# An LSTM step in which the residual part of h comes from a scan, the whole h is formed on GpSimd, and the output gate's sums change places

## What is computed

```
xW = einsum('ntd,dg->ntg', x, Wx) + b           # g = 2048 columns: i, f, o, g
a = xw_t + prev_h @ Wh
i, f, o = sigmoid(a[:, 0:H]), sigmoid(a[:, H:2H]), sigmoid(a[:, 2H:3H]);  g = tanh(a[:, 3H:])
next_c = f * prev_c + i * g
next_h = o * tanh(next_c)
x = x + hs
```

## Time and profile before

| what | value |
|---|---|
| median of three runs | 7913.7 us (7913.2 to 7918.02) |
| the profiled execution: its own time | 7913.46 us |
| its span | 7911.4 us |
| TensorE busy | 5366.3 us (68%) |
| VectorE busy | 5627.1 us (71%) |
| ScalarE busy | 2281.7 us (29%) |
| GpSimd busy | 842.9 us (11%) |
| granted TensorE clock in the LSTM steps (500 to 4000 us) | 1.00 |

### The profile page before, as it was taken

One profiled execution on the slowest core, in us unless ns is written; L12 is line 12 of the kernel. 1 busy time (PEld: TensorE's weight loads), 2 busy tenths in 40 slices (PEclk: granted clock), 3 DMA queues, 4 the chain that ended last, 5 costly groups with the idle time before them and its releaser, 6 DMA issues. The chain is left out here.

```text
span 7911.4 us, 404450 instructions
## 1 busy us (share of the span) xinstructions
PE 5366.3 (68%) x169280; PEld 4157.3 (53%) x169280; DVE 5627.1 (71%) x37427; ACT 2281.7 (29%) x12741; POOL 842.9 (11%) x2143
## 2 busy tenths in 40 slices
PE   1566666666666666666983666666666666666666
PEld 1455555555555555555431555555555555555555
DVE  7777777777777777777678777777777777777776
ACT  4322222222222222222354222222222222222222
POOL 5100000000000000000013000000000000000000
PEclk5899999999999999999996999999999999999999
DMA  2000000000000000000001000000000000000001
GB/s 85 17 0 0 0 0 0 0 0 0 0 0 0 0 0 0 0 0 0 0 0 43 0 0 0 0 0 0 0 0 0 0 0 0 0 0 0 0 0 43
DMA packets 32261, 37.24 MB, mean 5 GB/s; under 512 B 6112, under 2 KB 22496, under 8 KB 32224
## 3 DMA queue, kind: packets, MB, share of 16 engines
q1 hardware_dynamic: 32224, 36.76, 1.4%
HBM read 28.34 MB, written 8.39 MB: 5 GB/s over the span
## 5 line engine op out<-in xcount | busy, mean ns | idle before, releaser
L404 PE MATMUL q_PA<-scratch,q_H 128*8 128x256 f16 (+1 forms) x32768 | 1255.2, 273 | 1071.8 <-DVE q_H L619 1071.8
L404 PE MATMUL p_PA<-scratch,p_H 128*8 128x256 f16 (+1 forms) x32768 | 1254.9, 273 | 1071.8 <-DVE p_H L619 1071.8
L404 PEld LDWEIGHTS q_PA<-scratch,q_H 128*8 128x8 f16 (+1 forms) x32768 | 649.7, 90 | 1494.2 <-DVE q_H L619 1359.7
L404 PEld LDWEIGHTS p_PA<-scratch,p_H 128*8 128x8 f16 (+1 forms) x32768 | 649.0, 90 | 1494.6 <-DVE p_H L619 1359.6
L404 PE MATMUL q_PB<-scratch,q_H 128*8 128x256 f16 (+1 forms) x32768 | 1249.7, 273 | 0.0
L404 PE MATMUL p_PB<-scratch,p_H 128*8 128x256 f16 (+1 forms) x32768 | 1249.4, 273 | 0.0
L593 DVE STREAM_TRANSPOSE q_GT<-q_PA 128x192 f32<-128x192 f32 (+1 forms) x2048 | 526.0, 295 | 747.7 <-PE q_PA L404 747.7
L593 DVE STREAM_TRANSPOSE p_GT<-p_PA 128x192 f32<-128x192 f32 (+1 forms) x2048 | 526.5, 295 | 746.7 <-PE p_PA L404 746.7
L404 PEld LDWEIGHTS q_PB<-scratch,q_H 128*8 128x8 f16 (+1 forms) x32768 | 834.5, 92 | 59.8
L404 PEld LDWEIGHTS p_PB<-scratch,p_H 128*8 128x8 f16 (+1 forms) x32768 | 833.5, 92 | 60.8
L492 ACT ACTIVATE q_GBA<-q_PREA 128x24 f32<-128x24 f32 x1024 | 194.7, 190 | 1900.9 <-DVE q_PREA L598 1900.9
(11 more groups left out here) (220 smaller groups left out, 9390.6 us busy)
## 6 DMA issues: line engine op xcount, KB each, us to landing
scratch<-in_x_dram SPq DMA_DIRECT2D x8, 1024.0 KB, 5.4
out_dram<-xa SPq DMA_DIRECT2D x16, 512.0 KB, 6.1
xb<-in_L_cond_Wx_dram SPq DMA_DIRECT2D x8, 384.0 KB, 6.8
xb<-in_L_cond_Wh_dram SPq DMA_DIRECT2D x8, 384.0 KB, 6.7
xa<-in_L_cond_Wx_dram SPq DMA_DIRECT2D x8, 384.0 KB, 5.9
xa<-in_L_cond_Wh_dram SPq DMA_DIRECT2D x8, 384.0 KB, 6.1
xb<-in_L_cond_Wx_dram SPq DMA_DIRECT2D x8, 128.0 KB, 7.0
xb<-in_L_cond_Wh_dram SPq DMA_DIRECT2D x8, 128.0 KB, 6.8
```

The source lines that it names most:

```text
L404: last = nc.tensor.matmul(half.banks[buf][Q * j:Q * j + rows, 0:GA * Q], H[:, u, k, 0:rows], w16[:, part, k, j, half_cols(half)], start=False,
```

## The change

The sums of the output gates change places. The first half's o and the second half's g, i, f are neighbours in GT, and the two `both_parts` on them (8 and 24 elements) become one with 32, into one PSUM bank (PREB); the sigmoid of the first half's o now waits for it. The second half's o is transposed and summed ahead of the first half's high part, into PREA, with a wait for the transposition between the two (`to_b`).

`whole_h` leaves VectorE. The sigmoid of o and tanh of c are now written by ScalarE into one SBUF tile SO, in triples of which the first element is 0, the second the sigmoid and the third tanh of c; the element that was in PSUM before (tanh of c) is in SBUF now. H becomes HP, also in triples with -128 in the first element. `low_h` is a scan over 24 elements in place of an operation on 8: its state is multiplied by SO and HP is subtracted, so that after the first element of a triple it is 128, after the second 128 o, and after the third 128 o tanh(c) minus the high part. The matmuls read the third elements, 12 bytes apart, instead of adjacent columns. GpSimd multiplies the two parts of SO of four steps into HH, waits for that, and then adds HH to x.

The diff, without the renamed memsets, the allocation of the semaphores and the rewritten arguments of the calls:

```diff
-        H = sbt("H", [P, V, NC, Q], F16)
-        HH = sbt("HH", [P, 2, V, NC * B])
+        HP = sbt("H", [P, 2, V, V, 2, B, NF, 3], F16)
+        SO = sbt("SO", [P, U, 2, B, NF, 3])
+        HH = sbt("HH", [P, V, NC * B])
...
-                self.tanh_c = pst("TC" + name)[:, 0:M]
-                self.sig_o = sbt("SIGO" + name, [P, M])
+                self.n = chunk // NF
+                self.sig_o, self.tanh_c = (SO[:, :, self.n, :, :, e].rearrange("p u b c -> p u c b") for e in (1, 2))
...
+        first.pre_o, pre_o_and_gif, o_and_gif = second.pre[:, 0:M], second.pre[:, 0:4 * M], (first.o[0], second.gif[1])
+        second.pre_o = first.pre[:, 3 * M:4 * M]
...
-                    nc.gpsimd.tensor_tensor(here, here, HH[:, v].rearrange("p u (c b) -> p c u b", b=B), ALU.add).then_inc(s["xadd"], 1)
+                    nc.gpsimd.tensor_tensor(HH[:].rearrange("p u (h c b) -> p (u h) b c", h=2, b=B),
+                                            *(SO[:, v * V:(v + 1) * V, :, :, :, e].rearrange("p u h b c -> p (u h) b c") for e in (1, 2)), ALU.mult).then_inc(s["whole"], 1)
+                    pool.wait_ge(s["whole"], done)
+                    nc.gpsimd.tensor_tensor(here, here, HH[:].rearrange("p u (c b) -> p c u b", b=B), ALU.add).then_inc(s["xadd"], 1)
...
-                    last = nc.tensor.matmul(half.banks[buf][Q * j:Q * j + rows, 0:GA * Q], H[:, u, k, 0:rows],
+                    last = nc.tensor.matmul(half.banks[buf][Q * j:Q * j + rows, 0:GA * Q], HP[:, k // NF, u, 0:u + 1, :, :, k % NF, 2].rearrange("p u s b -> p (u s b)"),
...
-            nc.vector.memset(H[:], 0.0).then_inc(s["zero"], 1)
+            nc.vector.memset(HP[:].rearrange("p h s u t b c e -> p (h s u t b c) e")[:, :, 0], -H_SCALE).then_inc(s["zero"], 1)
+            nc.vector.memset(HP[:].rearrange("p h s u t b c e -> p (h s u t b c) e")[:, :, 1:3], 0.0).then_inc(s["zero"], 1)
...
-            def whole_h(half, v, u):
-                return nc.vector.tensor_tensor(HH[:, v, u, half.cols], half.sig_o[:], half.tanh_c, ALU.mult)
...
-                nxt = next_h(half, u)
-                return nc.vector.scalar_tensor_tensor(nxt[:, :, B:2 * B], by_unit(HH[:, v, u, half.cols]), H_SCALE, nxt[:, :, 0:B],
-                                                      ALU.mult, ALU.subtract)
+
+                here = (u + 1) % V
+                threes = lambda a: a.rearrange("p b c e -> p (b c e)")
+                return nc.vector.tensor_tensor_scan(threes(HP[:, half.n, here, here, 1]), threes(SO[:, v * V + u, half.n]),
+                                                    threes(HP[:, half.n, here, here, 0]), 0.0, ALU.mult, ALU.subtract)
```

More of the change, by code:

```diff
@@ L493, in steps @@
                                              scale=half_scale).then_inc(s["g_a"], 1)
-                        act.wait_ge(s["preo_a"], now)
-                        nc.scalar.activation(first.sig_o[:], first.pre_o, ACT.Sigmoid, scale=scale)
+                        act.wait_ge(s["pre_b"], now)
+                        nc.scalar.activation(first.sig_o[:, u], by_unit(first.pre_o), ACT.Sigmoid, scale=scale)
                         act.wait_ge(s["c_a"], now)
-                        nc.scalar.activation(first.tanh_c, first.c, ACT.Tanh, scale=0.5).then_inc(s["tc_a"], 1)
-                        act.wait_ge(s["pre_b"], now)
+                        nc.scalar.activation(first.tanh_c[:, u], by_unit(first.c), ACT.Tanh, scale=0.5).then_inc(s["tc_a"], 1)
                         nc.scalar.activation(second.tanhs, second.pre_gif.rearrange("p (n m) -> p n m", n=3), ACT.Tanh,
@@ L501, in steps @@
                         act.wait_ge(s["preo_b"], now)
-                        nc.scalar.activation(second.sig_o[:], second.pre_o, ACT.Sigmoid, scale=scale)
+                        nc.scalar.activation(second.sig_o[:, u], by_unit(second.pre_o), ACT.Sigmoid, scale=scale)
                         act.wait_ge(s["c_b"], now)
-                        nc.scalar.activation(second.tanh_c, second.c, ACT.Tanh, scale=0.5).then_inc(s["tc_b"], 1)
+                        nc.scalar.activation(second.tanh_c[:, u], by_unit(second.c), ACT.Tanh, scale=0.5).then_inc(s["tc_b"], 1)
             act.wait_ge(s["usual"], 1)
@@ L629, in _ @@
                         transposed(first, v, first.gif).then_inc(s["tr_a"], 1)
-                        transposed(first, v, first.o).then_inc(s["to_a"], 1)
+                        transposed(first, v, first.o)
                         dve.wait_ge(s["tr_a"], now)
@@ L636, in _ @@
                         multiply(first).then_inc(s["pr_a"], 1)
[L637 to L638 removed]
+                        dve.wait_ge(s["tr_b"], now)
+                        both_parts(pre_o_and_gif, u, o_and_gif).then_inc(s["pre_b"], 1)
                         dve.wait_ge(s["pr_a"], now)
                         new_c(first).then_inc(s["c_a"], 1)
[L641 to L642 removed]
                         transposed(second, v, second.o).then_inc(s["to_b"], 1)
+                        dve.wait_ge(s["to_b"], now)
+                        both_parts(second.pre_o, u, second.o).then_inc(s["preo_b"], 1)
                         dve.wait_ge(s["tc_a"], now)
[L645 to L646 removed]
+                        high_h(first, v, u).then_inc(s["hi_a"], 1)
                         dve.wait_ge(s["g_b"], now)
                         multiply(second).then_inc(s["pr_b"], 1)
[L649 to L650 removed]
                         dve.wait_ge(s["hi_a"], now)
@@ L655, in _ @@
                         dve.wait_ge(s["tc_b"], now)
-                        whole_h(second, v, u)
-                        high_h(second, u).then_inc(s["hi_b"], 1)
+                        high_h(second, v, u).then_inc(s["hi_b"], 1)
                         dve.wait_ge(s["hi_b"], now)
```

34 lines of the change are left out of this document (13 added, 21 removed).

## The result

The changed kernel takes 7976.4 us (median of four runs, 7975.4 to 7977.3), the kernel before on the same chip 7914.0. The ratio is 1.0079, 95% interval 1.0066 to 1.0091: slower by 62 us, 0.8%, where 7902 and a range to 7975 were forecast.

A forecast was written before the change was run, and what follows sets the result against it. The prediction took the kernel to be bound by 2048 repeats of one step's closed chain, with two routes ending together. From 7913.46 us, -41 (steps), +26 (GpSimd collisions) and +3 (ends) gave 7902 us, range 7835 to 7975.

The forecast's parts named there:

- The circle: The closed chain of one LSTM step, repeated 2048 times: 3.45 us for an ordinary step, and no engine the bound.
- two routes: First half's h plus 0.76 us of matmuls, and second half's h, both ending at 2.78 before TensorE's second batch.
- GpSimd collisions: VectorE held by GpSimd's instructions in first steps of groups: 0.10 us more in eight steps, 26 us lost.
- per step 0.02, and 2048 x 0.02 = 41 us: Gain of the whole step, the smaller of the two routes' gains: 0.02 us, 41 us over the run.
- First half: 0.06 - 0.04 - 0.01: First half's h: scan starts 0.06 us earlier, lasts 0.04 longer, first weight load costs 0.01; 0.02 gained.
- Gain 0.05, so this route isn't the bound: Second half's h: scan starts at 2.48 and ends at 2.68 us, against 2.73 before.
- In the mean 20: 0.01: TensorE's first weight load from columns 12 bytes apart, 20 columns in the mean at 0.56 ns each: 0.01 us lost.
- the ends: Ends of both LSTMs, a later last sum with x and larger memsets: together 3 us lost (0 to 6).
- the rival with a fixed part of its own: Rival on the short scan: from 0.22 us on no gain; at 0.23, 7962 us; chance 0.10.
- GpSimd's hold for its whole 0.32: Rival: GpSimd holds VectorE for its whole instruction, 0.52 us in eight steps less 0.11, +105 us: 7980 us; chance 0.12.
- The cheap ScalarE: Rival: tanh of c into SBUF lasts 0.18 us and strides cost nothing, gain 0.05 a step: 7840 us; chance 0.27.
- Spaced columns as TensorE's pace: Rival: spaced loads slow TensorE's groups by 0.012 us each, 0.13 in one step of four: 7970 us; chance 0.06.

The follow-up runs named there:

- the tanh experiment: Kernel before with only tanh of c written to adjacent elements in SBUF instead of PSUM: 8062.0 us, ratio 1.0182.

## Why the prediction was wrong

The circle, its two routes and the GpSimd collisions were read rightly. The step that failed is the term "per step 0.02, and 2048 x 0.02 = 41 us" gained. It asked for a gain of 0.03 on the poorer route before the loads' 0.01. The runs show none that lasts, and it fails in three places.

*"First half: 0.06 - 0.04 - 0.01" (the first half's route).* The scan starts 0.059 before the low part of before (means of the ordinary steps), as forecast, but it lasts 208 ns against 159, so that 0.012 are left at TensorE's start, without any load's price: less than half of the 0.03. The forecast had "0.01 to 0.02" here and took the upper end.

*"Gain 0.05, so this route isn't the bound" (second half).* It gains nothing. The new c started 0.01 earlier and lasted shorter, tanh of c started at 2.04 in the mean as forecast; then the row goes: tanh of c 219 ns (forecast 200), high part 187 with 33 to the scan (forecast 200 together), scan 208 (200). The high part starts at 2.30 instead of 2.28, the scan at 2.52 instead of 2.48, and it ends at 2.73 instead of 2.68. By the means of this half, 110 ns were saved (whole h 80, and the new c 12 earlier and 18 shorter), and the three instructions left in the chain became longer by 39, 31 and 41, which is 111. I had priced tanh of c (0.02) and the scan (0.04), and nothing for the high part, both of whose operands are now in SBUF and whose output is 12 bytes apart. The distance is worth 20 ns on that instruction (176 against 156 in the kernel before with 12 bytes); the other 11 are its inputs, of which the tanh experiment shows 3 to 5 for a tanh in SBUF (159 or 160 against 155 or 156). The rest stays unexplained; the inputs' own spacing is an obvious candidate that was not tried apart. Where the loads are adjacent, this route holds TensorE with 8 and 16 columns, and its loads come late with all; so goes what the first half had gained (0.003 and 0.005 a step, above).

*"In the mean 20: 0.01" (weight loads).* The row behind it was float32 with 128 columns, 0.56 ns a column. Spaced float16 costs up to 0.8 ns a column here (26 ns for 32). "Only the first load is exposed" comes close in the kernel before: a load becomes 1, 10, 18 and 26 ns longer with 8 to 32 columns, and the stretch between the batches 6, 14, 21 and 29. In the changed kernel some ns more are lost behind the second batch, whose loads follow a wait too. Measured 36 and 41 us, where 0.01 a step was 20. The forecast's own sign of being wrong, a second batch more than 0.77 after the first, came true with 0.772 to 0.804.

The sum with what was measured, by ratios: the route of h with the ends 0.9959 - 0.9963, -3 us with an interval of over 10 us to either side, where the forecast without its load term was -58; the loads +41 instead of +20; the collisions +24 instead of +26. Together +62, which is the result. The ends took 6 us where 3 were forecast. The miss of 74 us is 55 for the route and 21 for the loads, less 2 for the collisions.

Point by point, from the forecast's own list. Tanh of c started at 1.28 (forecast 1.30) and lasted 0.22 (0.20). The scan started at 1.75 and lasted 0.208 (1.74, 0.20), which bears out the price from the scan of 1024 elements; the rival with a fixed part of its own is out. The second half's o was summed at 1.44 (1.43), and the high part started at 1.53 (1.54), 0.03 after tanh of c had ended, so that no cost of the wait shows. The ordinary step is 3.45 to 3.49, not 3.42 to 3.43. The first steps are 0.07 and 0.16 longer than an ordinary one.

Of the rivals, GpSimd's hold for its whole 0.32 would have given 7980, close to the time, by another mechanism. It is refuted: the sum that starts 0.01 behind GpSimd is held for 0.16 and the multiply 0.12 behind it for 0.05, both until about 0.17 after GpSimd's start, and putting GpSimd off gave back 53 us and not the 133 that 0.52 in eight steps would have been. The cheap ScalarE (7840) fell with the tanh experiment: the row of 203 ns was the right one, and eight elements take 208. What the Trainium skill says (ScalarE: Activation LUTs, Step-by-step: what each stage is for), that PSUM is nearer to ScalarE, agrees with 180 against 208 ns for tanh of c, whose input is in SBUF; the sigmoid of o writes to SBUF in 177, but reads PSUM. Spaced columns as TensorE's pace was nearest in kind: with 16 columns and more they do set the pace between the two batches, by 0.014 to 0.029 a step, and not by the 0.13 of a step with 32 columns that the spacing of the earlier trace rows had given.

## What to carry to other kernels

When an instruction is taken out of a chain, price again every instruction that stays in it, for where its operands now lie and how far apart: here one instruction went that was worth 80 ns, and three others of 0.16 to 0.18 us became longer by 111 together. Work out each of two nearly equal routes to its end before one is called slack, since the gain is the smaller of the two. A gain that is the small rest of two larger terms, as 0.06 less 0.04 here, is within the error of either. And a helper engine's work is best placed by what its operands' port meets: one wait on GpSimd gave 53 us in the changed kernel and 29 in the one before, and with the moved sums of o it makes the best kernel here, 7868.7 us.

## What the runs showed of the hardware

- A load of 32 float16 columns takes 97 ns with columns 2 or 4 bytes apart, 107 with 8, 123 with 12 and 137 with 16; one of 8 columns 87, 87, 87, 88 and 92. The excess grows with the columns.
- A VectorE instruction that writes 8 float16 elements (the high part) takes 156 ns with the elements 2 or 4 bytes apart, 167 with 8, 175 with 12 and 185 with 16. That a write of eight elements could show its spacing was the surprise.
- ScalarE's tanh of 8 float32 elements in SBUF takes 180 ns into PSUM and 208 into SBUF; its sigmoid from PSUM into SBUF 177, and 184 with the elements 24 bytes apart. A VectorE product of 8 elements takes 168 ns with both operands in SBUF and 163 with one in PSUM.
- A scan takes 208 ns for 24 elements and 2.28 us for 1024.
- A VectorE instruction with two SBUF operands is held until 0.17 to 0.19 us after the start of a GpSimd instruction of 64 elements and 0.32 us, and not for the whole of it; one that starts 0.23 behind is not lengthened.
